# Hybrid attention / FFN / Mamba block on one core: thirteen woven streams in the attention, within-chunk products in fours, output added channel-major

## The reference

```python
q = short_conv(h @ Wq, conv_q); k = short_conv(h @ Wk, conv_k); v = short_conv(h @ Wv, conv_v)   # 4 taps, silu
g = exp(-softplus(h @ Wfa @ Wfb + dt_bias) * exp(A_log)); beta = sigmoid(h @ Wb)
q = l2norm(q) * DK ** -0.5; k = l2norm(k)
def step(S, inp):                       # over the tokens, S is 128 x 128 for each head and batch
    S = S * g_t; delta = (v_t - k_t @ S) * b_t; S = S + outer(k_t, delta); return S, q_t @ S
o = o * rsqrt(mean(o * o) + EPS) * norm_w * sigmoid(h @ Wga @ Wgb)
x = x + o.reshape(B, T, H * DV) @ Wo
```

## Time and profile before

| | us |
|---|---|
| median of three runs | 3273.89 |
| the profiled execution | 3279.82 |
| its span, first to last instruction | 3278.0 |
| the attention in it (L338 of the first unit to L894 of the last) | 57.7 to 2258.3 |
| PE busy, DVE busy in the span | 2752.0, 2310.1 |
| mean granted clock of PE, as a share of full speed | 0.92 |

### The profile page before, as it was taken

The page is one execution under the profiler, slowest core; times in us unless marked ns, Lnnn a source line. Parts: engine busy times, 40 slices in busy tenths (PEclk is TensorE's granted clock), DMA queues, the critical chain, the costliest instruction groups (busy, mean ns, idle before and its releaser), DMA issues.

```text
span 3278.0 us, 120319 instructions
## 1 busy us (share of the span) xinstructions
PE 2752.0 (84%) x54992; PEld 1687.9 (51%) x54992; DVE 2310.1 (70%) x3353; ACT 1339.1 (41%) x2525; POOL 1435.4 (44%) x1245
## 2 busy tenths in 40 slices
PE   6788888888888888898888898877888777787887
PEld 3565666566666666666666666664333322232333
DVE  3677777777777777777877787762367697776772
ACT  3343444344444444444443443432444334343331
POOL 0543454444444444444543444440066555665550
PEclk8899999999999999989988999987998889988999
DMA  1000000000000000000000000010022222222220
GB/s 53 11 12 11 17 14 11 11 17 14 11 12 17 13 11 11 11 17 14 11 12 11 17 14 11 6 45 21 1 89 88 78 89 87 78 88 84 94 77 13
DMA packets 52139, 106.74 MB, mean 33 GB/s; under 512 B 7084, under 2 KB 11948, under 8 KB 51376
## 3 DMA queue, kind: packets, MB, share of 16 engines
q1 hardware_dynamic: 51632, 99.04, 9.3%
HBM read 96.65 MB, written 2.37 MB: 30 GB/s over the span
## 4 chain that ended last, share of the span: by engine, by line
PE 63%; DVE 17%; issue 12%; ACT 6%; POOL 1%; DMA 0%; DVEq 0%; ACTq 0%; SPq 0%; POOLq 0%
PE bank L338 10%; PE bank L417 7%; DVE hs L1694 5%; PE bank L1529 4%; PE bank L411 3%; PE pair L574 3%; PE pair L560 3%; DVE acc L884 2%; PE bank L595 2%; PE bank L579 2%; PE pair L1464 2%; PE bank L525 2%; PE bank L516 2%; PE bank L347 2%; PE pair L1454 2%
## 5 line engine op out<-in xcount | busy, mean ns | idle before, releaser
L656 DVE SCALAR_TENSOR_TENSOR cv<-raw,taps,cv 128x1024 f32<-128x1024 f32 x288 | 455.8, 1583 | 18.6 <-ACT cv L949 18.4
L1947 POOL TENSOR_TENSOR dBu<-dtu,Bn 128x512 f32<-128x512 f32 x256 | 382.5, 1500 | 117.7 <-DVE hs L1694 114.1
L1529 PE MATMUL bank<-hc,eye 128*128 128x512 f32 x512 | 299.2, 684 | 131.1 <-DVE hc L1700 129.8
L1216 POOL TENSOR_TENSOR kL<-kL,tot 128x512 f32<-128x512 f32 x128 | 164.9, 1288 | 515.4 <-PE bank L411 515.4
L338 PE MATMUL bank<-xn,W 128*128 128x512 f32 x768 | 386.8, 635 | 0.5 <-issue 0.5
L948 ACT ACTIVATE raw<-bank 128x512 f32<-128x512 f32 x192 | 114.9, 598 | 529.4 <-PE bank L338 529.4
L1862 ACT ACTIVATE bank<-dtv,m_A 128x512 f32<-128x512 f32 x256 | 170.9, 686 | 229.2 <-DVE hs L1694 215.0
L1529 PEld LDWEIGHTS bank<-hc,eye 128*128 128x128 f32 x512 | 95.5, 207 | 308.9 <-DVE hc L1700 242.8
L1190 POOL TENSOR_TENSOR R<-qn,gate 128x1024 f32<-128x1024 f32 x32 | 76.4, 2388 | 302.6 <-ACT gate L1015 302.6
L338 PEld LDWEIGHTS bank<-xn,W 128*128 128x128 f32 x768 | 138.0, 196 | 136.2 <-issue 132.0
L1700 DVE TENSOR_TENSOR hc<-hs,Cn 128x512 f32<-128x512 f32 x256 | 198.7, 776 | 8.8
(11 more groups left out here) (254 smaller groups left out, 6286.0 us busy)
## 6 DMA issues: line engine op xcount, KB each, us to landing
Bn<-ssm_rows SPq DMA_DIRECT2D x128, 256.0 KB, 3.5
Cn<-ssm_rows SPq DMA_DIRECT2D x128, 256.0 KB, 3.2
W<-in_head_w SPq DMA_DIRECT2D x32, 448.0 KB, 3.2
WO<-in_out_w SPq DMA_DIRECT2D x32, 192.0 KB, 2.3
xT<-in_xT SPq DMA_DIRECT2D x1, 2048.0 KB, 8.1
out_xT<-xT SPq DMA_DIRECT2D x4, 512.0 KB, 3.5
xn<-in_w_gate SPq DMA_DIRECT2D x1, 1024.0 KB, 6.2
xn<-in_w_up SPq DMA_DIRECT2D x1, 1024.0 KB, 8.8
```

The source lines that it names most:

```text
L656: dve.scalar_tensor_tensor(cv[m % 2][:, :, :], raw[m % 2][:, :, i:i + SEG], taps[:, h, KQV[n], i:i + 1], cv[m % 2][:, :, :], MUL, ADD).the ...
L1529: pe.matmul(psum[Y_BANKS[jj]][:, :], eye[:, :], hc[(u * ITEMS + i) % AHEAD][:, :], start=False, stop=n == NS - 1, skip_group_check=True).t ...
L1947: pool.tensor_tensor(dBu[at % AHEAD][:, :], dtu[s][:, j, :], Bn[at // DT2 % DEEP][:, :], MUL).then_inc(dBu_set.sem)
```

## The change

Thirteen generators for each engine take the place of three: `conv(0)`, `conv(1)`, `conv(2)`, `dots`, `gating`, `turn_v`, `products`, `inverse`, `turn_k`, `solved`, `out_gate`, `state` and `output`. Each has a lag in units and its own table of places, all streams of all units stand on one scale (100 for a unit), and `braid` takes the next part of the lowest place, so no step ends anywhere. The products within a chunk (L579) are no longer issued chunk by chunk but eight calls at a time after chunks 3 and 7; `d` is written over `vT` so that it is still there then, and only the first chunk of four starts the accumulation in the bank `OUT`. `acc` is gone: the gated output is multiplied by `rstd_o` on DVE before it is turned (one instruction of 128x1024), the output weight is the stationary side (four matmuls of 512 columns), and each unit adds its product to `xT` (four DVE instructions of 128x512 of the form of L894). The low-rank product of the gate (L321 with `wfa`), which stood ahead of the first projection of a segment, now stands at the head of `gating`, behind `dots`. ScalarE loads a table three times a unit instead of twice (ahead of the tanh, of the first silu and of the norms' logarithm). The core of the diff; the other engines' generators are divided in the same way:

```diff
-FRONT_AT = [0, 4.1, 11.1, 16.4, 21.7, 26.9, 32.2, 38, 41.1, 47.5, 52.5, 58.5, 63.8, 69, 74.3, 79.6, 84, 95.3, 96.1]
-TREE_AT = [0, 2.6, 5.3, 7.9, 10.5, 13.2, 15.8, 18.4, 21.1, 23.7, 29.9, 29.9, 31.6, 33.2, 35.7, 39.5, 42.1, 44.3, 46.9,
-            49.2, 49.2, 56.9, 58.2, 61.3, 63.9, 66.5, 75.2, 75.2, 78.3, 78.3, 83.4, 89.9, 94.5, 94.5, 99.9, 99.9, 99.9,
-            99.9]
-STATE_AT = [6.7, 11.4, 11.4, 15.3, 16.1, 16.1, 27.8, 32, 36.1, 41, 45.7, 49.9, 57.2, 59.6, 65.5, 69.7, 73.9, 78, 79.1, 88,
-            93, 93, 93, 93]
+PLACES = [
+    (0, [-1, 7.3, 19, 20.5, 26.9, 34.4]),
+    (0, [18.6, 27.2, 35.2, 42.1, 51.2, 58.1]),
+    (0, [40.1, 51.1, 52.9, 52.9, 59.8, 61.8]),
+    (0, [57.5, 62.1, 70.7, 83.3]),
+    (0, [66.3, 66.3, 70.5, 83.1, 83.8, 94.9]),
+    (0, [83, 89.7]),
+    (1, [1.4, 1.4, 2.9, 5.9, 12.5, 18.2, 28.2, 37.2, 41.7, 46.7, 57.2, 67.1, 73.2, 75.4, 78.4]),
+    (1, [13.2, 31.6, 33.3, 35.8, 39.7, 44.3, 47, 49.3, 49.4, 57.2, 59.8, 63.8, 67.2, 76.6, 76.6, 78.5, 81.5,
+         83.6, 83.9, 89.9, 94]),
+    (1, [78.5, 82.8, 83, 83]),
+    (1, [102.2, 102.5, 103.2]),
+    (2, [14.6, 16.3]),
+    (2, [10.5, 15.5, 16.4, 16.5, 20, 24.3, 29.2, 33.5, 35.6, 47.4, 51.7, 57.3, 59.8, 65.6, 69.9, 74, 78.4,
+         78.4]),
+    (2, [40.1, 40.1, 77.9, 79.2, 79.4, 82.3, 82.3, 89, 89.2, 93.2, 93.2, 98.2, 104]),
+]
 LN_EXP, SILU_TANH = "natural_log_exp_and_others", "silu_and_others"
 
 
...
-    live = [[steps, places, 0] for steps, places in streams]
+    live = [(places[0], n, 0) for n, (steps, places) in enumerate(streams)]
     while live:
-        stage = min(live, key=lambda it: it[1][min(it[2], len(it[1]) - 1)])
-        stage[2] += 1
-        if next(stage[0], live) is live:
-            live.remove(stage)
+        at, n, k = min(live)
+        live.remove((at, n, k))
+        steps, places = streams[n]
+        if next(steps, streams) is not streams:
+            live.append((places[min(k + 1, len(places) - 1)], n, k + 1))
...
-        def att_drive(front, tree, state):
-            for step in range(NG + 2):
-                streams = []
-                if step >= 2:
-                    streams.append((state(step - 2), STATE_AT))
-                if 1 <= step <= NG:
-                    streams.append((tree(step - 1), TREE_AT))
-                if step < NG:
-                    streams.append((front(step), FRONT_AT))
-                braid(streams)
+        wo_full, x_added = tally("wo_full", 4), tally("x_added", 4)
+
+        def att_drive(*stages):
+
+            streams = []
+            for g in range(NG):
+                for stage, (lag, places) in zip(stages, PLACES):
+                    streams.append((stage(g), [100 * (g + lag) + at for at in places]))
+            braid(streams)
 
...
-                                  skip_group_check=True)
+                        pe.matmul(psum[OUT][rows_of(b), (c % 4) * P:(c % 4 + 1) * P], R[s][:, 1, c, b, :], src[:, b, :],
+                                  start=c % 4 == 0, stop=False, skip_group_check=True)
                     yield
                     pe.wait_ge(*d_set.at(g, c))
                     for b in range(NB):
-                        m = pe.matmul(psum[CHAIN[b]][:, P:2 * P], kT[s][rows_of(b), c, :], d[c % 2][rows_of(b), :])
+                        m = pe.matmul(psum[CHAIN[b]][:, P:2 * P], kT[s][rows_of(b), c, :], vT[g % 3][rows_of(b), c, :])
                     m.then_inc(outer_full.sem)
-                    if c == 0:
-                        pe.wait_ge(*at_set.at(g))
-                    for b in range(NB):
-                        m = pe.matmul(psum[OUT][rows_of(b), oc], AT[s][rows_of(b), c, :], d[c % 2][rows_of(b), :],
-                                      start=False, stop=True, skip_group_check=True)
-                    m.then_inc(within_full.sem)
-                    if c == 5:
-                        turn_out(g, 0)
-                    yield
-                yield
-                turn_out(g, 1)
-                yield
-                for n in range(4):
+                    yield
+                    if c % 4 == 3:
+                        if c == 3:
+                            pe.wait_ge(*at_set.at(g))
+                        for c4 in range(c - 3, c + 1):
+                            for b in range(NB):
+                                m = pe.matmul(psum[OUT][rows_of(b), (c4 % 4) * P:(c4 % 4 + 1) * P],
+                                              AT[s][rows_of(b), c4, :], vT[g % 3][rows_of(b), c4, :], start=False,
+                                              stop=True, skip_group_check=True)
+                        m.then_inc(within_full.sem)
+                        if c == 3:
+                            yield
+
+            def output(g):
+                s = g % 2
...
                     bank = take()
-                    if n == 0:
-                        pe.wait_ge(*wo_scaled.at(g))
-                    if n % 2 == 0:
-                        pe.wait_ge(*ogT_set.at(g, n // 2))
-                    for i in range(2):
-                        m = pe.matmul(psum[bank][:, i * HID:(i + 1) * HID], WT[s][:, 2 * n + i, :], WO[s][:, P:P + HID])
-                    m.then_inc(wo_full.sem)
-                    held[bank] = acc_set.at(g, n)
-                    yield
-                if h == H - 1:
+                    if hh == 0:
+                        pe.wait_ge(*og_scaled.at(g))
+                    for c in range(4 * hh, 4 * hh + 4):
+                        m = pe.transpose(psum[bank][:, (c % 4) * P:(c % 4 + 1) * P], og[:, c, :], eye[:, :])
+                    m.then_inc(og_turned.sem)
+                    held[bank] = ogT_set.at(g, hh)
+                    yield
+                for hh in range(2):
                     for k in range(KT):
-                        for a2 in range(2):
-                            bank = take()
-                            pe.wait_ge(*acc_set.at(g, 3))
-                            for c in range(4 * a2, 4 * a2 + 4):
-                                m = pe.transpose(psum[bank][:, (c % 4) * P:(c % 4 + 1) * P],
-                                                 acc[:, c, k * P:(k + 1) * P], eye[:, :])
-                            m.then_inc(acc_turned.sem)
-                            held[bank] = x_added.at(seg, 2 * k + a2)
+                        bank = take()
+                        if k == 0:
+                            pe.wait_ge(*ogT_set.at(g, hh))
+                            if hh == 0:
+                                pe.wait_ge(*wo_scaled.at(g))
+                        pe.matmul(psum[bank][:, :], WO[s][:, (k + 1) * P:(k + 2) * P],
+                                  WT[s][:, 4 * hh:4 * hh + 4, :].rearrange("p c n -> p (c n)")).then_inc(wo_full.sem)
+                        held[bank] = x_added.at(g, 2 * hh + k)
+                        if 2 * hh + k < 3:
                             yield
 
...
                         dve.wait_ge(*u_set.at(g, 1))
-                    dve.tensor_tensor(d[c % 2][:, :], vT[g % 3][:, c, :], psum[CHAIN[0]][:, 0:P], SUB).then_inc(d_set.sem)
+                    dve.tensor_tensor(vT[g % 3][:, c, :], vT[g % 3][:, c, :], psum[CHAIN[0]][:, 0:P],
+                                      SUB).then_inc(d_set.sem)
...
                 dve.scalar_tensor_tensor(osum[:, :], norms[g % 3][:, NC:2 * NC], 1e-6 * P * P, osum[:, :], MUL,
                                          ADD).then_inc(o_var.sem)
                 yield
-                for n in range(4):
-                    bank = turn.next()
-                    if n == 0:
...
+                for hh in range(2):
+                    turn.next()
+                    yield
...
+                        bank = turn.next()
+                        dst = half_cols(xT[:, k, :].rearrange("p (b t) -> p b t", b=NB), seg, hh)
+                        dve.wait_ge(*wo_full.at(g, 2 * hh + k))
+                        if g:
+                            dve.wait_ge(*x_added.at(g - 1, 2 * hh + k))
+                        dve.tensor_tensor(dst, dst, psum[bank][:, :].rearrange("p (c b t) -> p c b t", b=NB, t=CH),
+                                          ADD).then_inc(x_added.sem)
+                        if 2 * hh + k < 3:
                             yield
 
-            att_drive(front, tree, state)
+            att_drive(conv(0), conv(1), conv(2), dots, gating, turn_v, products, inverse, turn_k, solved, out_gate, state,
```

711 lines of the change are left out of this document (327 added, 384 removed).

## The result

| | before | after |
|---|---|---|
| median, same chip | 3269.89 us (4 runs) | 3222.39 us (4 runs) |
| ratio, 95% interval | 1 | 0.9849, 0.9819 to 0.9878 |
| the profiled execution, its span | 3279.82, 3278.0 | 3223.97, 3222.0 |
| attention from the unit's line to its last start, a unit | 67.24 us | 65.58 us |
| PE's issue waits, its waits for data, a unit | 5.93, 2.23 us | 5.07, 2.26 us |

The change makes the kernel 47 us or 1.5% faster. The forecast was 27 us. The sign and the range were right, the size was not.

A forecast was written before the change was run, and what follows sets the result against it. PE was taken to set the pace, 87% busy in the attention. 31 units x (-1.0 + 0.25 + 0.1) = -20, and -7 once, make -27 us: 3247 us, range 3178 to 3308 (the forecast's own 3225 to 3265).

The forecast's parts named there:

- Denser blocks: PE's issue waits: the batch packs its instructions into less time, more blocks fall short of 3.4 us; +0.25 us a unit.
- the floor: PE's instruction fetch: a block of 256 PE instructions needs at least 3.4 us, whatever is in it.
- the average over all starts: PE's blocks: time missing to 3.4 us, averaged over every pass as start; 7.5 us a unit before, 7.8 in the new order.
- The batch: Within-chunk products on PE, sixteen passes in a row at 59 ns each: -1.0 us a unit, bounds 0 and -1.2.
- Rival B: PE's fetching takes the batch's saving back as pauses, only -7 us stays: 3267 us, no change; chance 0.15.
- The output: Output product, four 512-column matmuls for sixteen passes: 0 on PE, and DVE keeps its load.
- the waits ahead of the transposes: PE at the output, behind squares, gating, root, scaling and DVE's copies: +0.8 us of new waits a unit.
- Waits for data: PE's waits for other engines: -1.25 us go, 1.35 come, net +0.1 us a unit, bounds -1.5 and +3.
- rival A: DVE paces the state chain, waits for data rise 2.5 us a unit: 3321 us, slower; chance 0.25.
- its sign of 1.5: PE's waits at L573 for vT: if these alone pass 1.5 us a unit, DVE paces the chain and the forecast is wrong.
- rival C: The weave closes nearly all PE waits for data, and fewer stops give back 0.25 us of low clock: 3174 us; chance 0.15.
- Once only: Start and end of the attention: gate's low-rank product -3, turning of acc -2, end chain -2; together -7 us.

The follow-up runs named there:

- the gate moved: Changed kernel with the gate's first 512-column product put ahead of chunk 5's outer product instead of behind chunk 6's prediction: 3177.21 us, 0.9677 to the kernel before.

## Why the prediction was off

**The step that failed: "Denser blocks", +0.25 us.** It had the batch pack its instructions into less time, so that the issue waits rise, from 5.9 to 6.2 us a unit. They fell, by 0.86 and 0.43 in the two profiles of the changed kernel. They are lower with the batch than without it in each pair of kernels: 5.57 against 5.93 in the old order, 5.53 against 5.93 in the streams with the old output, 5.07 and 5.50 against 5.90 in the changed kernel, 5.80 against 5.97 with the gate moved. The streams alone left them at 5.93. The term is off by 0.7 to 1.1 us a unit, 21 to 34 us, and the forecast by 20. Two things in its working were wrong.

First the floor. "At least 3.4 us, whatever is in it" was read from one block of the earlier trace rows. (No record is missing there: 127 passes and two semaphore instructions are the 256.) The kernel before has this too:

```profile
1159.52 3.70 PE L338 MATMUL bank<-xn,W 128*128 128x512 f32 x8
...
1163.74 0.76 PE L411 MATMUL bank<-R,kL 128*32 128x32 f32 x64
1164.43 0.75 PE L417 MATMUL bank<-XY,Bc 32*32 32x32 f32 x64
1165.11 0.49 PE L574 MATMUL pair<-d,kT 64*128 64x128 f32 x4
...
1168.36 0.27 PE L417 MATMUL bank<-XY,Z 32*32 32x32 f32 x9 [1.25 <-issue]
```

Behind long projections 128 passes go by in 1.37 us (1163.74 to 1165.11) without a pause, and the next pause comes at 1168.36. Of 353 blocks from 300 to 2100 us 21 took under 3.0 us, each behind a block of 4.3 us or more. So a dense block behind a long one can go without its pause. My sum charged each block by itself, which may be why it had 7.5 us where 5.9 are measured.

Second the average over all starts. In the old order they pass through all positions and it is right. With 3333 instructions a unit they don't, and the place counts: shifting both kernels by half a block leaves 18 of the 47 us, somewhat under my 27. So about 29 us hang on the place, and the forecast's being near at the other place is partly luck, since the term was wrong there too: issue waits fell from 6.25 to 5.71 between the shifted kernels. Two positions were timed, not all. Why the issue waits fall with the batch stays open; in the changed kernel the waits for data and the low clock rise in their place.

**The batch, -1.0.** The work was right (-0.83). Its worth wasn't: 2 to 6 us in the changed kernel, 9 in the old order, 19 in the streams with the old output, 24 with the gate moved, each with 10 to 15 us of uncertainty. In the first the waits for data and the low clock are higher with the batch than without it; that the two take back its work is the reading that fits, since its worth came back where the clock held. Rival B had this result and another cause.

**The output, 0.** Alone it costs 145 us. In the streams the kernels that have it are 19 to 34 us faster, with the place of the blocks not separated from it, so 0 may be right there. My estimate of the waits ahead of the transposes (+0.8 with those behind them, before a third was taken off) stands against 0.54 for L598 and L387. I had no term for the parts working on each other.

**Waits for data, +0.1.** Measured +0.03 and, in the second profile, -0.11. The waits are where they were expected (L568 gone, L573 longer), and rival A did not come, though L573's 1.33 us a unit is near its sign of 1.5. (By its own sum A is even with no change at +1.0, not +1.1.) The longest wait, 0.8 to 0.9 us a unit at chunk 5, is the one I had at 0.7.

**The clock** stood in the sum nowhere but in rival C. Its mean hardly moved in the change (0.920 to 0.923 in the profiles), though the time at the lower level goes from 3.6 to 14.7 us a unit between the kernels of the table.

**Once only, -7.** The start came 5.2 us earlier (79.7 to 74.5; 77.3 in the second profile), 3 were forecast. From the last L439 or L415 to the attention's end it is 101 us in place of 94, where I had -2. In the drain:

```profile
2192.50 1.97 PE L581 MATMUL bank<-vT,AT 64*64 64x128 f32 x16
2200.19 1.94 PE L598 MATMUL bank<-eye,cen 128*128 128x128 f32 x8 [5.73 <-DVE cen L854]
2202.01 5.61 PE L609 MATMUL bank<-WT,WO 128*128 128x512 f32 x8
```

The chain that the streams hide stands open once, 5.73 us, and the clock is low, so L609 takes 5.61 us in place of 3.8. From L581 to the end it is 15.9 us, where it was 14.2 and 11.7 were forecast. The other 5 us of the growth lie ahead of it, and no run shows their cause.

## What to carry to other kernels

When PE runs stretches of small matmuls, count its instructions a period. Near a multiple of 256 the pauses move little from period to period; here 128 instructions far ahead were worth 1%. So an order, or one part of it that changes the count, should be timed in two positions before it is judged. Put long matmuls where PE both pauses and waits for another engine: here that held the clock up and was worth 61 us, more than the whole change. Work taken off PE paid less here where a wait for DVE and a fall of the clock stood close behind it.

## What the runs showed of the hardware

Pauses of PE for which the trace shows no cause stood at one place of a count of 256 instructions from the start of its queue, in all three kernels counted: 128 instructions in front moved them, against the work, by half a block. In a series by itself a block took 3.2 to 4.0 us with 1.9, 2.5 or 3.3 us of work in it, and 3.73 at either level of the clock; behind a long block 128 dense passes took 1.37 us without a pause. Behind 4 us in which PE was busy 1.60, the granted clock was 0.59 for the next 8; behind 4 us with 2.66 it stayed 1.00. A DVE instruction more a unit cost 9 us in all at one place and 49 at another.
